# A fused attention and expert layer: the softmax denominators asked for one tile later, and one output projection put ahead of a group's last ones

## The reference, cut to what matters

```python
qkv = einsum(x, Wqkv_w) + Wqkv_b          # q: 512, k: 32, v: 32
scores = einsum('bqhd,bkd->bhqk', q, k) * 32 ** -0.5, causal
attn = softmax(scores); ctx = einsum('bhqk,bkd->bqhd', attn, v)
x = layernorm(x + ctx @ out_w.T + out_b)
x = layernorm(x + experts(x))             # top 2 of 8: (silu(x w1) * (x w3)) w2, weighted
```

## Time and profile before

| | |
|---|---|
| median of 3 runs | 1225.65 us |
| profiled execution | 1230.7 us, of which span 1228.6 us |
| TensorE (PE) matmul busy | 1111.8 us, 90% |
| VectorE (DVE) busy | 892.7 us, 73% |
| ScalarE (ACT) busy | 712.2 us, 58% |
| GpSimd (POOL) busy | 163.9 us, 13% |
| mean granted TensorE clock | 0.961 |
| shares of the chain that ended last | PE 70%, DVE 18%, issue 6% |

### The profile page before, as it was taken

One profiled execution on the slowest core, in us unless ns is written; L12 is line 12 of the kernel. 1 busy time (PEld: TensorE's weight loads), 2 busy tenths in 40 slices (PEclk: granted clock), 3 DMA queues, 4 the chain that ended last, 5 costly groups with the idle time before them and its releaser, 6 DMA issues.

```text
span 1228.6 us, 18308 instructions
## 1 busy us (share of the span) xinstructions
PE 1111.8 (90%) x6080; PEld 528.5 (43%) x6080; DVE 892.7 (73%) x1095; ACT 712.2 (58%) x828; POOL 163.9 (13%) x153
## 2 busy tenths in 40 slices
PE   5389999998999999998988998999899999999886
PEld 4137433743335543333732743374333454333252
DVE  3155688768887589888576668866888767988756
ACT  4253468336884477886336347833688446788611
POOL 4220121102001011001004003110200101100000
PEclk9689999999999999998999999999899999999978
DMA  9901540163001450001064163016300145000000
GB/s 215 223 23 45 128 104 1 35 138 103 2 1 36 105 137 1 2 1 35 10 131 106 36 137 104 2 35 138 103 2 1 36 90 117 1 2 1 2 1 35
DMA packets 65680, 74.41 MB, mean 61 GB/s; under 512 B 14224, under 2 KB 48016, under 8 KB 65552
## 3 DMA queue, kind: packets, MB, share of 16 engines
q1 hardware_dynamic: 49968, 58.74, 18.9%
q0 software_dynamic: 13584, 11.54, 6.2%
q10 hardware_dynamic: 2000, 2.51, 0.7%
HBM read 25.58 MB, written 8.39 MB: 28 GB/s over the span
## 4 chain that ended last, share of the span: by engine, by line
PE 70%; DVE 18%; issue 6%; SPq 2%; ACT 1%; DMA 1%; POOL 1%; DVEq 1%; ACTq 0%; POOLq 0%
PE sc L1053 18%; PE bank L1075 15%; PE sc L943 10%; DVE psum_k L743 10%; PE sc L1192 7%; PE bank L943 7%; PE sc L1093 4%; PE bank L1093 2%; PE sc L1207 2%; SPq L364 2%; DVE stats L819 2%; DVE res L816 1%; PE sc L1138 1%; PE bank L1200 1%; DVE res L826 1%
## 5 line engine op out<-in xcount | busy, mean ns | idle before, releaser
L577 ACT ACTIVATE prob<-sc 128x1024 f32<-128x1024 f32 x544 | 525.5, 1025 | 168.9 <-PE sc L1053 158.3
L743 DVE TENSOR_TENSOR psum_k<-psum_k,prob 128x2048 f32<-128x2048 f32 x170 | 395.7, 2327 | 5.9 <-ACT prob L577 0.8
L1053 PE MATMUL sc<-q_st,k_st 128*128 128x512 f32 x1088 | 332.7, 426 | 30.5 <-DMA q_st<-q_lo 21.9
L1053 PEld LDWEIGHTS sc<-q_st,k_st 128*128 128x128 f32 x1088 | 185.4, 190 | 277.8 <-ACT prob L577 175.1
L1075 PE MATMUL bank<-prob,v_sb 128*32 128x512 f32 x2176 | 288.6, 606 | 0.0
L467 POOL TENSOR_SCALAR_AFFINE_SELECT prob<-prob 128x1024 f32<-128x1024 f32 x64 | 86.5, 1388 | 618.6 <-ACT prob L577 618.4
L1192 PE MATMUL sc<-prob,w_sb 128*128 128x512 bf16 x512 | 122.7, 383 | 2.9 <-DVE prob L892 2.9
L743 DVE TENSOR_TENSOR psum_k<-prob 128x2048 f32<-128x2048 f32 x28 | 64.1, 2289 | 69.3 <-ACT prob L577 65.3
L1075 PEld LDWEIGHTS bank<-prob,v_sb 128*32 128x32 f32 x2176 | 43.7, 108 | 106.5 <-issue 91.6
L943 PE MATMUL bank<-q_st,wq_hi 128*128 128x512 f32 x240 | 81.0, 402 | 0.0
L609 ACT ACTIVATE prob<-sc 128x512 f32<-128x512 f32 x64 | 37.3, 597 | 68.1 <-PE sc L1192 68.0
(11 more groups left out here) (127 smaller groups left out, 1019.1 us busy)
## 6 DMA issues: line engine op xcount, KB each, us to landing
q_st<-q_hi SPq DMA_DIRECT2D x128, 128.0 KB, 2.7
q_st<-q_lo SPq DMA_DIRECT2D x128, 128.0 KB, 2.8
res<-in_x SPq DMA_DIRECT2D x8, 1024.0 KB, 5.3
res<-ob_sb POOLq DMA_DIRECT2D x8, 1024.0 KB, 10.2
out_x<-res SPq DMA_DIRECT2D x32, 256.0 KB, 5.7
res<-in_xT SPq DMA_DIRECT2D x7, 1024.0 KB, 5.2
w_sb<-in_w POOLq DMA_DIRECT2D x8, 256.0 KB, 14.2
prob<-in_wqkvT ACTq DMA_DIRECT2D x4, 288.0 KB, 6.0
```

The lines of the kernel that those rows point to most:

```text
L577: nc.scalar.activation(prob[t % NP][:, half * HW:(half + 1) * HW], score_half(q // TB, 2 * t + half).rearrange("p m n -> p (m n)"), ACT.Ex ...
L743: nc.vector.tensor_tensor(acc[:, :], first[:, :], prob[t % NP][:, :], ALU.add).then_inc(add_v, 1)
L1053: last = nc.tensor.matmul(dst, k_st[:, k * P:(k + 1) * P], q_st[slot][:, c * HJ:(c + 1) * HJ, at:at + P], start=True, stop=not shift)
```

## The change

`DLAG` goes from 2 to 3. So TensorE runs `scores(LAST + 3)` and `times_values` of the tile before last ahead of a block's denominators, VectorE runs one more addition ahead of `normalise_context`, and the ring's order follows. In `finish_attention` on TensorE, `project_out(g, 0)` goes ahead of the group's last denominators.

```diff
-DLAG = 2
+DLAG = 3
...
                     if g == 0:
                         pe.wait_ge(ow_low, 1)
+                    project_out(g, 0)
                     denominators(TB * (g + 1) - 1)
-                    project_out(g, 0)
                     project_out(g, 1)
                     project_out(g, 2)
```

## The result

The changed kernel takes 1208.97 us, the median of 4 runs (1206.59 to 1209.90), against 1226.3 us before (4 runs, 1221.99 to 1229.3). The ratio is 0.9858, 95% interval 0.9825 to 0.9892: 17.3 us faster. I had forecast 1217.3 us and a range from 1212.5, so the direction was right and the gain twice as large. The profiled execution took 1208.3 us, its span is 1206.1 us, 22.5 us less than the one before.

What follows compares the result with a forecast made beforehand. TensorE was taken to bound the kernel, busy 90% of the span. First blocks -9.2, other blocks +0.8, group 0 and swap 0 sum to -8.4 us, giving 1217.3 us; forecast's own range 1214 to 1220.5, overall range 1212.5 to 1224.5.

Steps and rivals of the forecast that it cites:

- First blocks: Blocks 4, 8 and 12, both sequences: TensorE does one more tile before the denominators, limited by the ring slot; -9.2 us.
- here the wait of 2.63 us only moves to the slot: Block 4, second sequence: the slot frees at 754.55, scores started at 754.56 before; gain 0.
- the rest of block 8's wait: Block 8: 2.1 us of the 4.2 us wait remain; full clock assumed afterwards, gains 2.4 and 3.6 us.
- Other blocks: Blocks after a group's first: the ring slot comes 0.20 us later against TensorE; +0.8 us in sum.
- group 0: Block 0's denominators: +0.9 us behind the query-stack wait in sequence one, -0.9 us of slot wait in sequence two; together 0.
- The swap: Group ends: projection moves ahead of the last denominators, the "issue" wait stays and stands before it; 0 us.
- up to -1 us: Group 3's end: 8 projection matmuls cover more of the second "issue" wait than 8 denominator ones, per sequence.
- The whole wait goes: Rival, first blocks: the slot holds nobody, 17.5 us fall away, less 0.8; 1209 us, chance 6%.
- VectorE pays it back: Rival, blocks 4 and 8: only VectorE's idle time is a lasting gain, the next denominators wait again; 1223.5 us, 24%.
- The slower one: Rival, group ends: VectorE's residual chain comes 2.8 us later, nothing hides it, `turn_x1` waits; 1240 us, chance 6%.
- The group ends gain: Rival, group ends: the 3 us waits belong to the denominators, the projection fills them; 22 us more, 1195 us, 4%.

Runs made afterwards that it cites:

- the changed kernel moved back: Changed kernel plus 253 never-executed instructions in TensorE's branch for group 3, moving that group's end to number 200; 1222.46 us, ratio 0.9944 to the kernel before.
- the lag alone moved: Kernel before with DLAG = 3, no swap, plus 6 never-executed instructions moving group 3's end to number 206; 1208.31 us, ratio 0.9839.
- before, moved: Kernel before plus 24 never-executed instructions in TensorE's branch for group 3, moving that group's end to number 206; 1222.93 us, ratio 0.9951.
- number 200: Jump target at group 3's end, counted modulo 256, just ahead of a supposed instruction-block border; DLAG = 3 alone 1220.65 us, changed kernel with 253 dead instructions 1222.46 us.
- the six past the border: Kernels whose group 3 end lies behind a supposed border between instruction numbers 200 and 203, the changed kernel among them; 1198.73 to 1222.93 us.

## Why the prediction was wrong

- *First blocks, -9.2 us.* The mechanism was right: the additions' wait fell to 4.9 us, the slot was free at A + 5.25, and the groups of blocks 8 and 12 gained 2.4, 0.8, 3.5 and 1.1 us where I had 2.4, 0.8, 3.6 and 0.8. At block 4 I had 1.6 and 0; the profiles show -0.2 and -1.7. What was missing is in "here the wait of 2.63 us only moves to the slot": it moves, and behind 2.19 us at the slot half clock followed in both sequences. I had asked what the rest of block 8's wait would do to the clock, and not asked it of block 4's new one. But part of this is the luck of two executions. With the changed kernel moved back (both sequences) and the lag alone moved (the first) the clock stayed full, and the group's tiles took 97.2 to 97.5 us; where it fell, 98.7 to 99.1. Before, they took 98.8 and 97.3.
- *Other blocks, +0.8 us, and group 0, 0 us.* Block 9's slot wait went from 0.22 to 0.41 us, as forecast. The group 0 terms stayed below what can be told.
- *The lag in all.* By runs it gave 5.4 us (2 to 9) in one pair (1 - 0.9956) and some 14 us (9 to 19) in the pair with the code moved (0.9839 against 0.9951). The forecast of 8.4 lies between. The profiles say that it was about right: all tile stretches together took 867.0, 871.3 and 867.3 us in the three kernels with `DLAG = 2`, and 857.9 to 860.9 in the five with `DLAG = 3` and VectorE's work at the same lag, 8.6 us less on average.
- *The swap, 0 us.* Right: the four pairs of kernels that differ in it agree within their intervals. My "up to -1 us" for covering the second wait was too little in one profile: with the swap alone 0 and 0.9 us of it were left. Past the border there is nothing to cover.
- *The step that failed:* "In group 3 a second such wait comes 8 matmuls later; [...] so up to -1 us in each sequence." I had the wait in the trace and the rule that it belongs to, and still priced it as fixed, something that work could only cover. It depends on where the code lies, and the change moved that by 21 instructions. It was worth 4.4 and 4.5 us in the profile (the wait of 2.2 or 2.0, and the half clock behind it). By runs the place of the code alone is worth 6.0 us (before, moved), 10.5 us (changed, moved back) and 14.4 us (lag alone, 0.9956 to 0.9839). The two ends of group 3 together took 58.5 us in the profile before, 58.7 and 62.2 in the two kernels at number 200, and 49.6 to 52.9 in the six past the border. With the 8.9 us of this pair the sum is -8.4 - 8.9 = -17.3 us. That it meets the runs to a tenth is luck: the other five kernels past the border have 5.6 to 6.8 us less than before, not 8.9.
- *The rivals.* Of the named ones none came. "The whole wait goes" named 1209 us, the time that was measured, but what it says did not happen: the scores waited 9.9 us for the slot. "VectorE pays it back" is out: the gain lasts. The slower one is out: `turn_x1` waited 4.5 us once, 0.5 more than before, in the last group. "The group ends gain" had the right place and the wrong cause.

## What to carry to other kernels

Where an engine waits for "issue" behind a jump, count its instructions up to the target before believing that an edit's time is its own: an edit that moves code can gain or lose more than the edit, and a control with dead instructions separates the two. When a wait is taken away from a consumer, put the work that frees the resource ahead too: VectorE had to ask at the old place for TensorE's later one to pay in full. And a wait that only moves is not free: half clock can follow it at the new place as at the old one, and not in every execution.

## What the runs showed of the hardware

The jump out of the `If` cost TensorE 2.4 to 3.0 us at each of the changed kernel's eight group ends. A target 1 to 3 instructions ahead of the border cost 6.0 to 6.4 us, one about 20 ahead of it 2.5 + 2.2 and 2.9 + 2.0 us. That the border comes again after 256 instructions is borne out by one run: 253 more of them brought a target from just behind one border to just ahead of the next, and the wait was 6.3 us again. 24 or 6 instructions that never run were worth 6.0 and 14.4 us. Half clock followed a TensorE wait of 2.2 us in seven of ten places, one of 2.0 us in two of fourteen.
